# Semaphore increments of TensorE's products, pair products and ring slots moved onto drains of its queue, in a graph attention layer

## What is computed

```python
h_src = nfeats[src]
h_dst = nfeats[dst]
z_att = jnp.concatenate([h_src, h_dst, efeats], axis=-1)
e = jax.nn.leaky_relu(z_att @ W_attn + b_attn, negative_slope=0.01)[:, 0]
m = jnp.concatenate([h_src, efeats], axis=-1) @ W_ne
emax = jax.ops.segment_max(e, dst, num_segments=N)
ex = jnp.exp(e - emax[dst])
denom = jax.ops.segment_sum(ex, dst, num_segments=N)
alpha = ex / denom[dst]
z = jax.ops.segment_sum(alpha[:, None] * m, dst, num_segments=N)
out = jax.nn.relu(jnp.concatenate([nfeats, z], axis=-1) @ W_out)
# the caller: x = _layernorm(x + out, axis=-1)
```

## Time and profile before

| | us |
|---|---|
| median of 3 runs | 4999.54 |
| lowest, highest | 4994.14, 5000.15 |
| the profiled execution's own time | 4990.13 |
| its span, first to last instruction | 4988.3 |

### The profile page before, as it was taken

One profiled execution on the slowest core, in us unless ns is written; L12 is line 12 of the kernel. 1 busy time (PEld: TensorE's weight loads), 2 busy tenths in 40 slices (PEclk: granted clock), 3 DMA queues, 4 the chain that ended last, 5 costly groups with the idle time before them and its releaser, 6 DMA issues.

```text
span 4988.3 us, 64221 instructions
## 1 busy us (share of the span) xinstructions
PE 2010.8 (40%) x9870; PEld 1926.7 (39%) x9871; DVE 2579.2 (52%) x4868; ACT 2315.7 (46%) x4121; POOL 2978.3 (60%) x3149
## 2 busy tenths in 40 slices
PE   1444444434343334443434333434333433343346
PEld 0334444433333333333433333433333333343346
DVE  5555455555554555555555555545555555555556
ACT  1455555444444444444444444444444444444444
POOL 6566666666666666666666666656666666666651
PEclk9666666666666666666666666666666666666666
DMA  5444444444444444444444444444444444454441
GB/s 111 122 130 126 128 129 132 128 129 129 127 127 128 130 129 130 130 127 124 131 128 127 127 130 130 130 129 128 126 129 127 129 129 130 123 136 128 126 129 53
DMA packets 759570, 628.92 MB, mean 126 GB/s; under 512 B 608412, under 2 KB 608796, under 8 KB 759332
## 3 DMA queue, kind: packets, MB, share of 16 engines
q1 hardware_dynamic: 646164, 519.51, 36.2%
q0 software_dynamic: 100096, 102.60, 11.1%
q10 hardware_dynamic: 13072, 4.80, 0.5%
HBM read 621.58 MB, written 4.81 MB: 126 GB/s over the span
## 4 chain that ended last, share of the span: by engine, by line
issue 31%; another core or an unknown queue 17%; ACT 17%; DVE 15%; DVEq 10%; ACTq 7%; PE 1%; POOL 0%
ACT zb L508 4%; ACT psE L507 4%; DVE prod L619 3%; DVE u L623 3%; DVEq L741 2%; ACTq L513 2%; ACT acc L471 2%; DVE um L728 2%; ACT pT L461 2%; DVE acc L682 2%; ACT psS L499 2%; DVE e L689 1%; DVEq L708 1%; ACT ebias L502 1%
## 5 line engine op out<-in xcount | busy, mean ns | idle before, releaser
L365 POOL DMA_INDIRECT V<-in_x_dram,srcs x3128 | 2953.4, 944 | 1883.4 <-PEq L892 951.2
L851 PE MATMUL psT<-ident,e 128*128 128x128 f32 x3136 | 757.9, 421 | 2593.2 <-ACT pT L461 1249.6
L851 PEld LDWEIGHTS psT<-ident,e 128*128 128x128 f32 x3136 | 615.5, 219 | 2664.2 <-issue 2399.5
L857 PE MATMUL psG<-V,pT 128*128 x6288 | 1237.3, 379 | 13.4 <-DVE acc L682 11.2
L857 PEld LDWEIGHTS psG<-V,pT 128*128 128x128 f32 x6288 | 1232.3, 299 | 15.3 <-issue 15.2
L461 ACT COPY pT<-psT 128x512 f32<-128x512 f32 x784 | 434.0, 579 | 1348.6 <-remote 1301.4
L619 DVE TENSOR_TENSOR prod<-V,psM 128x1024 f32<-128x1024 f32 x391 | 477.6, 1221 | 828.0 <-issue 827.9
L728 DVE CUSTOM_DVE_ANT_0 um<-ubc,psS 128x1024 f32<-128x1024 f32 x391 | 476.5, 1219 | 617.1 <-issue 315.6
L623 DVE TENSOR_REDUCE u<-prod 128x8 f32<-128x1024 f32 x391 | 477.0, 1220 | 62.5 <-issue 22.4
L689 DVE TENSOR_TENSOR e<-zb,psE 128x1024 f32<-128x1024 f32 x392 | 475.5, 1213 | 10.6 <-issue 8.0
L499 ACT ACTIVATE psS<-dbc,nbias 128x1024 f32<-128x1024 int32 x391 | 437.0, 1118 | 12.8
(11 more groups left out here) (95 smaller groups left out, 656.3 us busy)
## 6 DMA issues: line engine op xcount, KB each, us to landing
ubc<-scores SPq DMA_DIRECT2D x391, 512.0 KB
dbc<-in_dst_dram SPq DMA_DIRECT2D x390, 512.0 KB
V<-in_edge_attr_dram SPq DMA_DIRECT2D x390, 256.0 KB
V<-in_x_dram,srcs POOLq DMA_INDIRECT x3128
scores<-u SPq DMA_DIRECT2D x391, 4.0 KB
srcs<-in_src_dram SPq DMA_DIRECT2D x390, 4.0 KB
out_dram<-y SPq DMA_DIRECT2D x12, 256.0 KB
xt<-in_x_dram ACTq DMA_DIRECT2D x6, 448.0 KB
```

Of the source, the lines that this page charges most:

```text
L365: nc.gpsimd.indirect_dma_start(V[0:n, s, j, 0:F], None, x[:, :], bass.IndirectOffsetOnAxis(ap=srcs[0:n, s, j:j + 1], axis=0)).then_inc(h_i ...
L851: last = nc.tensor.transpose(psT[:, i, j * P:(j + 1) * P], e1[:, :].rearrange("q (p j) -> q j p", j=J)[:, 4 * i + j, :], ident[:, :])
L857: last = nc.tensor.matmul(psG[:, 0:AW], pT[:, i, j * P:(j + 1) * P], V[:, bass.ds(sv, 1), 4 * i + j, :].rearrange("p a f -> p (a f)"), sta ...
```

## The change

Three kinds of increment no longer hang on a matmul or on a plain increment of PE's queue, but on a `drain` instruction of that queue, which stands behind the work that it tells of.

- In `window` both `agg_half` and `agg_done` are incremented by two drains behind all eight products. The fourth product no longer increments anything.
- In `supertile` the wait for `agg_done` before the increment of `v_free` is gone; a drain carries `v_free`. It stands behind the register operations and the load of L890.
- In `y_pair` a drain behind the product carries `y_ready`.

The increments of `tr[0]` and `tr[1]` stay on the last transpose of their half. No work of any engine is added or removed otherwise, and the matmuls keep their order.

```diff
@@ y_pair
                 y_turn()
-                y_multiply().then_inc(y_ready, 1)
+                y_multiply()
+                pe.drain().then_inc(y_ready, 1)
@@ multiply
                 for j in range(4):
-                    last = nc.tensor.matmul(psG[:, 0:AW], pT[:, i, j * P:(j + 1) * P],
-                                            V[:, bass.ds(sv, 1), 4 * i + j, :].rearrange("p a f -> p (a f)"),
-                                            start=(i == 0 and j == 0), stop=(i == 1 and j == 3))
-                last.then_inc((agg_half, agg_done)[i], 1)
+                    nc.tensor.matmul(psG[:, 0:AW], pT[:, i, j * P:(j + 1) * P],
+                                     V[:, bass.ds(sv, 1), 4 * i + j, :].rearrange("p a f -> p (a f)"),
+                                     start=(i == 0 and j == 0), stop=(i == 1 and j == 3))
@@ window
                 multiply(0, sv)
                 multiply(1, sv)
+                pe.drain().then_inc(agg_half, 1)
+                pe.drain().then_inc(agg_done, 1)
@@ supertile
                 if ahead:
                     pe.load(coming, trip[0:1, bass.ds(2 * t + 3, 1)])
-                    pe.wait_ge(agg_done, pe.snap(g))
-                    pe.sem_inc(v_free[(s - BEHIND) % RING], 1)
+                    pe.drain().then_inc(v_free[(s - BEHIND) % RING], 1)
```

## The result

The changed kernel takes 5185.16 us (median of 4 runs, 5183.26 to 5190.79), the kernel before in the same comparison 4996.84 us (4993.93 to 5000.15, 4 runs): a ratio of 1.0379, with a 95% interval of 1.0361 to 1.0397. It is 3.8% slower. The profiled span grew from 4988.3 to 5181.4 us, by 193 us.

What follows compares the result with a forecast made beforehand. It took a circle as the bound: POOL's burst, PE's late increment, `v_free`, the next burst. Late drains would add 313 x 0.8 = 250 us to 4990, giving 5240 us; range 4480 to 5560, the likeliest case's own 5180 to 5300.

Steps and rivals of the forecast that it cites:

- case 1: PE's drains as late as the increments were, `v_free` 0.8 us later in 313 waits: 5240 us (5180 to 5300), chance 0.32.
- case 2: Drains prompt, transposes' increments late in long gather runs; every two windows become a pair: 4920 to 5070 us, chance 0.22.
- third case: Drains prompt at the products' end and little else late, POOL the bound: 4300 us, between 4039 and 4570, chance 0.27.
- `v_free`, 0.8 us later in 313 waits: Register work and load come behind the first drain, so POOL's next gather waits longer: 313 x 0.8 = 250 us.
- everything stays: If drains are late, nothing changes but `v_free`, 0.8 us later in an unchanged 313 waits of POOL.
- `agg_half`: Told at the eighth product instead of the fourth, some 1.7 us later; copy 0 hides that, cost nothing while covered.
- The drain of `y_ready`: Comes 49 times where PE has idle time; set at nothing, at most 40 us if late.
- the circle: POOL's burst of eight gathers, PE's late increment after it landed, `v_free`, next burst: 12.33 us a window.

Runs made afterwards that it cites:

- slots version: Kernel before with only `v_free` on a drain behind the load, without the wait for `agg_done`; products keep their increments: 4919.83 us, ratio 0.9976.
- version without a drain: Kernel before with PE's wait for `agg_done` moved right behind the products, ahead of the register work and load: 5055.14 us, ratio 1.0246.
- two versions with 0.318 us: Changed kernel with register work and load ahead of the two drains, ratio 1.0163; the same with `agg_half` back on the fourth product, ratio 1.0174.
- products alone: Changed kernel with `v_free` and `y_ready` as before, so only `agg_half` and `agg_done` ride on drains: 5107.49 us, ratio 1.0367.
- run 20: Not a label of a run: "run" is a run of POOL's gathers, and 20 counts windows of the kernel before told within 1 us.
- version with the dose: Kernel before with `v_free` on a drain and ten empty drains ahead of it; products' increments stay attached: 5069.58 us, ratio 1.0282.
- version with 128x990: Kernel before with POOL's own product over 128x990 elements behind each group's fourth gather: 4785.74 us, ratio 0.9701.

## Why the prediction was right, and where it was not

The forecast was 5240 us and slower, the measurement 5185 us: case 1 by its sign and by its mechanism, 55 us short of it in size, and just inside that case's own range (5180 to 5300). That it lies inside is in part luck: the size of the delay came out, the number of pauses didn't.

1. **Drains are as late as the increments.** Right, and shown: the drain of the slots version ends 33 ns behind the late attached increment, and in no window before it. The prediction had only weighed it. Cases 2 and 3 needed drains that are prompt where the increments are late; no such thing was seen. The sentence of the Trainium skill, "PSUM — Partial Sum Buffer", section "Engine vs sequencer instructions", that a drain waits for the engine to go fully idle, holds in the sense that the completion has to be in; read as "at the products' end", it would have given the third case.

2. **`v_free`, 0.8 us later in 313 waits.** The mechanism and the 0.8 us were right: `v_free` ends 0.84 us farther behind `agg_done`, and the second drain adds 0.11. What the pauses make of it must be summed from their means, since the single ones have short outliers that the medians hide. The mean single pause grew from 2.41 to 3.08 us and the pair's from 3.92 to 5.08: with the old number and mix of pauses 263 x 0.67 + 58 x 1.15 = 243 us, close to the 250 forecast. The count didn't stay: 321 pauses became 269, since POOL ran through two groups 110 times instead of 58, and a pair has one pause of 5.08 us where two singles have 2 x 3.08 = 6.16. That gave the other 56 us back, which leaves 187. The step that was off is "everything stays", the count of 313 waits: 250 us forecast for 187 measured.

3. **More pairs.** The prediction had laid them to prompt drains (case 2, "every two windows a pair"). The version without a drain has 119 of them, so they need no drain. That a later `v_free` makes them isn't shown as a rule: the two versions with 0.318 us have 85 and 60, and the slots alone, with no later `v_free`, 73. How pairs come about stays open.

4. **`agg_half`.** Set at nothing; moving it back changed the ratio from 1.0163 to 1.0174, nothing. Right.

5. **The drain of `y_ready`.** Set at nothing, at most 40 us. The whole change (1.0379) and the products alone (1.0367) differ in it and in the drain of the slots, and their intervals overlap. Right, as far as that shows.

6. **What the profile would show.** Case 1 named a wait of ACT laid to PE's drains, which is there with 1291.1 us, and a wait of POOL of 3.85 us on average; it is 4.48, because pairs, whose pause is longer, have more weight.

7. **What bounds the kernel.** "PE's late increment, which comes only when the burst is over and landed" holds for "over": with four gathers and a long quiet it is prompt, with a gap in the burst it comes in the gap. Whether the gathers' landing matters isn't shown. What the prediction missed is that the circle can be opened at POOL's end. A drain was no quicker way to tell; the message needed quiet on POOL, in the right place and of the right length.

## What to carry to other kernels

In this kernel a drain was no quicker messenger than an increment attached to the matmul: it ended no sooner (33 ns later in most windows), and held the queue until then, so whatever stands behind it (register work, a load, the next products) comes later by its own length. Before an increment is moved, look what stands between it and the one that waits, and put that work ahead. Where a completion comes late, look at what the neighbour engines are doing at that moment before changing how it is told: here a deliberate gap of 1.85 us in POOL's burst of gathers gained 3.0%, where the change of messenger lost 3.8%.

## What the runs showed of the hardware

- TensorE's completions (attached increments and drains alike) are mostly held while POOL starts an indirect gather every 1.25 us. In the kernel before, of 163 windows whose last product started behind the fourth gather of a run 20 were told within 1 us; of 181 in which it started later in the run, none. With a long quiet behind every four gathers 377 of 378 were. The increments of ACT and DVE come 8 to 12 ns behind their instructions' ends, in the bursts too. TensorE itself isn't held either: transposes and products go on. Which part of the chip holds the message isn't shown by any run here.
- How long after the last gather's start a held message came differs: 2.5 to 2.9 us with the gap of 2.97 us (315 of the 322 in the gap), about 1.95 us (median) with the gap of 2.39 us, and at a median of 2.9 and 3.6 us in the kernels before and after.
- A gap of 2.97 us from start to start of two gathers let 322 of 375 messages out in it, and one of 2.39 us about half (178 of 369). One of 3.45 us let out 363 of 380 and gained nothing over none: it adds 2.2 us to a group, and the pauses that it replaces took 862 us in 380 groups, 2.27 us each.
- A drain behind an idle engine shows 8 to 13 ns (L893 and L876 of the changed kernel). Two in a row end 0.11 us apart there, and ten in a row add 0.07 us each in the version with the dose.
- POOL's product holds up a small operation of DVE. Beside the product of 1.85 us `wnode` takes 1450 ns on average where it took 235. The first line is of the kernel before, the second of the version with 128x990:

```profile
L718 DVE TENSOR_SCALAR wnode<-node,half 128x3 f32 x391 | 91.9, 235 | 490.4 <-issue 288.2
...
L730 DVE TENSOR_SCALAR wnode<-node,half 128x3 f32 x391 | 566.8, 1450 | 475.6 <-issue 421.5 <-DVE u L635 51.2 <-ACT zb L520 2.8
```

The 282 that overlap with POOL's product take 2012 ns (median), the other 109 take 229. The Trainium skill, "SBUF — State Buffer", section "Who interferes with whom", says that such an operation can take a mode with two ports, that the pair is shared with GpSimd, and that the later of the two is fully blocked; the trace agrees with these 2012 ns. The same section says that PE never waits on anyone. It speaks of the ports, and for PE's work the traces agree (379 ns a matmul record of the products before, 381 with the gap); the messages, late by 6.6 us (median of the late ones before, from the last product's start), lie outside of it. Whether a gap made of something that leaves DVE alone gains more wasn't tried.
